# Attention kernel: which pairs of max tiles VectorE reads with one instruction

## The reference

```
q, k, v = split_heads(x @ w.T * s + b)            # 8 x 16 heads x 1024 x 16
scores = einsum('bhqd,bhkd->bhqk', q, k) / sqrt(16)
attn = softmax(scores)                            # needs the maximum of each row of 1024 scores
ctx = einsum('bhqk,bhkd->bhqd', attn, v)
x = layernorm(x + ctx @ w_o.T * s_o + b_o)
```

## Time and profile before

| what | value |
|---|---|
| median of the runs | 1981.04 us |
| the profiled execution | 1983.3 us, span 1981.5 us |
| PE busy | 1931.0 us, 97% of the span |
| DVE (VectorE) busy | 1845.4 us, 93% |
| ACT (ScalarE) busy | 1652.1 us, 83% |
| granted TensorE clock | 0.997 of full speed |

### The profile page before, as it was taken

The page is one execution under the profiler, slowest core; times in us unless marked ns, Lnnn a source line. Parts: engine busy times, 40 slices in busy tenths (PEclk is TensorE's granted clock), DMA queues, the critical chain, the costliest instruction groups (busy, mean ns, idle before and its releaser), DMA issues.

```text
span 1981.5 us, 43034 instructions
## 1 busy us (share of the span) xinstructions
PE 1931.0 (97%) x15806; PEld 1131.4 (57%) x15806; DVE 1845.4 (93%) x3236; ACT 1652.1 (83%) x3241; POOL 750.0 (38%) x747
## 2 busy tenths in 40 slices
PE   8999999999999999999999999999999999999998
PEld 7766444444444444444444444444478888888876
DVE  4788999999999999999999999999289999999997
ACT  6655889899898989989898988988967777777776
POOL 3000364666575353010001001000046666666785
PEclk9999999999999999999999999999999999999999
DMA  7985553355435435433543544353011111111210
GB/s 224 284 236 209 120 76 52 62 95 96 94 81 102 95 80 99 93 94 82 101 96 78 97 94 94 82 100 98 28 49 49 49 49 49 49 49 56 63 33 27
DMA packets 127199, 181.46 MB, mean 92 GB/s; under 512 B 37836, under 2 KB 82636, under 8 KB 126988
## 3 DMA queue, kind: packets, MB, share of 16 engines
q1 hardware_dynamic: 119308, 171.10, 37.6%
q10 hardware_dynamic: 7392, 7.34, 1.1%
q0 software_dynamic: 288, 0.27, 0.1%
HBM read 103.68 MB, written 73.40 MB: 89 GB/s over the span
## 4 chain that ended last, share of the span: by engine, by line
DVE 63%; PE 32%; issue 3%; DMA 1%; ACT 1%; SPq 0%; DVEq 0%; POOLq 0%; POOL 0%; ACTq 0%
DVE halfmax L1135 50%; PE ps L1401 10%; DVE halfmax L1130 7%; PE ps L1440 6%; PE ps L494 4%; PE ps L504 3%; PE ps L1389 2%; PE ps L1412 2%; PE ps L1045 1%; PE ps L1011 1%; PE ps L481 1%; PE ps L1448 1%; DVE room L1591 1%; PE ps L1457 1%; DVE room L1678 1%
## 5 line engine op out<-in xcount | busy, mean ns | idle before, releaser
L1096 ACT ACTIVATE room<-ps 128x512 f32<-128x512 f32 x2048 | 1084.4, 600 | 125.0 <-PE ps L1011 103.0
L1135 DVE TENSOR_REDUCE halfmax<-ps 128x1 f32<-128x512 f32 x1714 | 1039.5, 676 | 1.3 <-PE ps L986 1.3
L1011 PE MATMUL ps<-qs,ks 50*128 50x512 f32 x2048 | 716.4, 448 | 2.4 <-DVE halfmax L1135 1.3
L986 PE MATMUL ps<-ks,qs 48*128 48x512 f32 x1960 | 667.6, 437 | 23.8 <-DVE halfmax L1130 22.3
L1045 PE MATMUL ps<-room,vals 128*17 128x256 f32 (+2 forms) x8192 | 578.9, 384 | 0.3 <-ACT craw L1104 0.3
L986 PEld LDWEIGHTS ps<-ks,qs 48*128 48x128 f32 x1960 | 314.5, 185 | 423.6 <-DVE halfmax L1135 309.2
L164 POOL CAST mrow<-turned_rows 128x32 fp32r<-128x32 f32 x32 | 6.7, 210 | 904.2 <-DVE turned_rows L159 695.4
L1011 PEld LDWEIGHTS ps<-qs,ks 50*128 50x128 f32 x2048 | 327.2, 184 | 22.9 <-ACT room L1096 14.5
L1045 PEld LDWEIGHTS ps<-room,vals 128*17 128x17 f32 x8192 | 167.4, 96 | 232.9 <-issue 168.1
L1401 PE MATMUL ps<-wguT,xqT 128*128 128x512 f32 (+1 forms) x1152 | 268.4, 386 | 3.9 <-DVE xqT L1631 3.9
L1401 PEld LDWEIGHTS ps<-wguT,xqT 128*128 128x128 f32 x1152 | 212.0, 189 | 51.8 <-issue 9.9
(11 more groups left out here) (116 smaller groups left out, 2212.1 us busy)
## 6 DMA issues: line engine op xcount, KB each, us to landing
qk_parts<-parts SPq DMA_DIRECT2D x64, 512.0 KB, 3.9
qs<-qk_parts SPq DMA_DIRECT2D x192, 128.0 KB, 4.4
ks<-qk_parts SPq DMA_DIRECT2D x192, 128.0 KB, 7.1
ctx_raw<-craw SPq DMA_DIRECT2D x64, 256.0 KB
ready<-passing SPq DMA_DIRECT2D x27, 512.0 KB, 6.5
pairs<-ready SPq DMA_DIRECT2D x27, 512.0 KB
out_dram<-fin SPq DMA_DIRECT2D x64, 128.0 KB, 1.7
xin<-in_L_attn_x_dram ACTq DMA_DIRECT2D x14, 512.0 KB, 5.4
```

The source lines that it names most:

```text
L986: nc.tensor.matmul(ps[:, MX + max_number(i, u, bank) % 4, :], qs[rows, i.slot(RING), pair, t * P:(t + 1) * P], ks[rows, i.slot(RING), pair ...
L1011: nc.tensor.matmul(ps[:, score_bank(i, s, n), :], ks[rows, slot, pair, kt * P:(kt + 1) * P], qs[rows, slot, pair, qh * BANK:(qh + 1) * BAN ...
L1096: nc.scalar.activation(prob[:, prob_slot(i, s), score_order(i, s)[n], :], ps[:, score_bank(i, s, n), :], ACT.Exp, scale=float(D) ** -0.5). ...
L1135: nc.vector.tensor_reduce(halfmax[:, i.slot(2), bank, column:column + 1], ps[:, at + bank, :], AX.X, ALU.max, negate=True).then_inc(max_re ...
```

## The change

A unit is now whole when its two max tiles are the second and third pair of a block of three. With the block layout above this is so for units 0, 4, 7, 10 and 13 of each 16 (before: 0 and 7): 306 units of 980 in place of 123. TensorE's instructions and their order stay as they are, only the counts that it waits for on `max_read` follow the new table.

```
-    WHOLE = (0, 7)
+
+    SECONDS = {tiles[1] for tiles, quarters in blocks() if len(tiles) == 3}

     def whole(i, u):

-        return item[i.k, u] % (2 * KT) in WHOLE
+        return GH + max_number(i, u, 0) in SECONDS
```

## The result

The changed kernel takes 1997.37 us (median of 5 runs, 1994.1 to 1997.9). On the same chip the kernel before took 1980.39 (5 runs). The ratio is 1.0077, with a 95% interval of 1.0059 to 1.0095: slower by 12 to 19 us. The forecast was + 14 and 1995 us. The span of the profiled execution went from 1981.5 to 1996.1, + 14.6, against 1995.6 in the prediction.

What follows compares the result with a forecast made beforehand. VectorE was taken to bound the attention, with TensorE and VectorE waiting in turn. Cycles of 21.66 + 3.73 + 3.84 + 9.72 made a 38.95 us group, +0.46 over 30.6 groups: +14.1, 1995 us, range 1989 to 2001.

Steps and rivals of the forecast that it cites:

- The bound: Attention: VectorE is the bound; back to back, a whole read saves 0.065 us over two single reads, not 140 ns.
- The plain cycles: Six cycles of six max tiles per group, whole read to whole read: 3.61 us each, against 3.59 read one by one.
- The cycles with the reciprocal and the turn: One cycle each per group, containing VectorE's reciprocal or the turn's transpose: 3.73 and 3.84 us; both let TensorE catch up.
- The transpose's wait: At the turn, no read stands between `whole_max` and the transpose waiting for it: a step of 0.23 us, against 0.10 if covered.
- The cycles of eight tiles: Two cycles per group, units 0 and 16 with a block of two behind: 4.72 us bare plus 0.14 stall, 4.86 each.
- TensorE's lost lead: In plain cycles TensorE writes a pair 0.56 us before its read, formerly 0.95; the missing 0.39 delays the eight-tile cycles.
- The sum: One group of 64 max tiles, reciprocal to reciprocal: 38.95 us against 38.49; over 30.6 groups, +14.1 us.
- Rival A: Whole reads cost only their own time, so VectorE gains 183 x 0.065 = 11.9 us: 1969 us, chance 0.05.
- The larger saving that the prediction names beside A: The Trainium skill's fixed PSUM read cost: one read for two saves 125 ns, about 23 us in all, 1958 us.
- B: Only plain cycles stall; eight-tile cycles get through and the transpose's wait is hidden: group 38.54, 1982.5 us, chance 0.10.
- C: Dense plain cycles fall behind further, each standing still once more by 0.14: group 39.79, 2021 us, chance 0.05.
- the idle time before the max matmul put down to the whole reads: Idle time before L987 put down to L1131 was to grow from 22.3 us, in many more but shorter pieces.

Runs made afterwards that it cites:

- the first test above: Whole units moved to the first and second pair of a block of three, against the changed kernel's second and third: 1967.94 us, 0.9928 of the kernel before.

## Why the prediction was right

**The bound.** That VectorE's reads set the pace, and that a whole read saves 0.065 us from start to start and not 0.14: with none whole the group is 38.66, with two 38.54. Right.

**The plain cycles.** 3.61 us forecast; 3.61 measured. This term carries the change: six cycles that each lose 0.09 where they would have saved 0.065. It could be worked out ahead of the change because the trace of before already held one such cycle, in the earlier trace rows, up to the place of the next whole read.

**The cycles with the reciprocal and the turn.** 3.73 and 3.84 forecast, 3.72 and 3.84 measured. The transpose's wait was 0.22 (0.23 forecast), and splitting that unit took it away.

**The cycles of eight tiles.** 4.86 forecast, 4.86 measured, the stall of 0.14 among it. This was the widest term (0 to 0.39). The account of it was TensorE's lost lead, passed on by ScalarE. The traces can be held against each other here. First ScalarE's copy of the values behind the whole read of 706.03 before, then three lines behind the whole read of 712.11 after:

```profile
706.51 0.62 ACT L1104 ACTIVATE craw<-ps 128x512 f32<-128x512 f32 x1
```

```profile
712.98 0.62 ACT L1105 ACTIVATE craw<-ps 128x512 f32<-128x512 f32 x1
...
714.63 0.18 PEld L1012 LDWEIGHTS ps<-qs,ks 50*128 50x128 f32 x1 [0.20 <-ACT room L1097]
...
715.83 0.49 PE L987 MATMUL ps<-ks,qs 48*128 48x512 f32 x1
```

The copy starts 0.87 us behind the start of the whole read in place of 0.48, the score tile 2.52 (714.63) in place of 2.13 (708.16 in the earlier trace rows), and the first max tile of the next block 3.72 (715.83) in place of 3.34 (709.37): 0.38 to 0.39 later each time, as forecast. And the score tile's weight load now waits 0.20 us for an exponential. In 243:1384 the table of waits has 58 such waits, two for each of 29 groups, where it had one before. So the trace shows the path through ScalarE as well as the size; no run took ScalarE's part away.

**The sum.** 38.95 a group against 38.98 measured, + 14.1 us against + 14.6 in the span and + 17 in the medians (12 to 19).

**Rival A** (full saving, 1969 us) had the right price and the wrong place: moved to the first and second pair, the same whole reads give 1968 us. That the two numbers are so near is in part luck, since that version also lifts the one stall of 0.09 us that the kernel before has in each group, and A's sum does not. The larger saving that the prediction names beside A, 125 ns a read and 1958 us, is not seen: whole reads save 0.06 to 0.065 us each. **B** and **C** did not come.

**What was wrong.** I wrote that the idle time before the max matmul put down to the whole reads would grow from 22.3 us. It fell to 6.9. The wait shows at the weight load in front of it, where the table of waits has 117.3 us in 244 waits for the whole reads, and had 74.9 us in 122 before. The two together grew from 97.2 to 124.2 us, so the wait grew as forecast, in more and shorter pieces (274 in place of 182), but not in the row that was named. The step from a unit's second tile to its read was also priced a little long, at 0.53 us: in the first test above 0.48 was enough. No term hangs on it: in the plain cycles of the changed kernel VectorE stands still for the first tile of the block, two reads earlier.

The durations of the reads rose by 4 ns (680 and 1216), where I had them unchanged. The starts, not the durations, carry the sum, so nothing follows from it.

## What to carry to other kernels

Where two engines hand buffers round in a ring, price a cheaper instruction by the loop it closes, not by its own time: add up release, waiting instruction, what is queued behind it, and first use, and compare with the time the other engine can fill. A larger read gives its buffers back later and all at once, so ask which instruction in the producer's order will wait for it, and put it where nothing long stands behind that one. Look in the trace of before for one place that already has the new pattern; compare n instructions in a row with n times the start-to-start distance, since a stall under the overlap of two records is listed nowhere.

## What the runs showed that I had not expected

Less work on TensorE made the kernel before 83 us slower. With half the value columns gone, its granted clock falls again and again from 1.00 to 0.50 in the attention, from the 2.4 to the 1.2 GHz level (0.916 over the whole execution); uncut it stays at 1.00. In the stretch ahead of such a fall, 461:480 above, TensorE is busy for 0.93 of the time, where the uncut kernel has 0.98. But the cut changed kernel is emptier still (913.86 of 1020 us, 0.90) and keeps the full clock through those 1020 us. It loses it at the two ends of the attention, 0.85 in 150:250 and 0.68 in 1370:1450, and that is why its execution is not as fast as its groups say. The Trainium skill, "TensorE: Matmul & The Clock Gate", Part 1, has the gate follow how busy TensorE has been. That goes with the fall as such; why the emptier of the two kernels is spared, neither it nor these runs show.
